# A two-layer graph attention kernel: one table of node products with three bf16 rows per node, one window load and one matmul per edge group, buffers 42 wide

## The chip, the cores and the metric

The kernel runs on one core of one Trainium2 chip. The metric is the device time of one execution in microseconds (us). TensorE is called PE, VectorE DVE, ScalarE ACT, GpSimd POOL and SyncE SP; PEld is PE's loading of weights. SP, ACT and POOL also issue DMAs.

## What is computed

A graph has 6250 nodes and 106250 edges (17 per node: 50000 random pairs in both directions, and one loop at each node). Edges are sorted by their target `dst`. Two attention layers follow one another, and the result is normalised. Cut to what matters:

```python
def egat(x, e, src, dst, W_ni, W_nj, W_fij, W_node, attn):
    f = (x @ W_ni.T)[src] + (x @ W_nj.T)[dst] + e @ W_fij.T      # per edge, 128 wide
    f = leaky_relu(f, 0.2)
    score = f @ attn
    a = softmax of score over the edges with the same dst
    return segment_sum((x @ W_node.T)[src] * a[:, None], dst), f

h0, h1 = egat(x, edge, src, dst, layer 1 weights)
h0 = relu(h0) + x;  h1 = relu(h1) + edge
h0b, _ = egat(h0, h1, src, dst, layer 2 weights)
out = layernorm(x + (h0b + x))
```

All inputs are f32.

## The kernel before, in words

Edges are cut into tiles of 128, groups of `TG` = 4 tiles (512 edges, `W`) and chunks of `GC` = 8 groups. There are 26 chunks (`CH`), 208 groups (`NG`) in each layer. Everything is kept transposed: features on the 128 partitions, edges along the row.

The stages are: (1) `project`, 13 slabs of 512 nodes: the product x @ W_nj, written to DRAM in bf16 parts; (2) layer 1; (3) `middle`, again 13 slabs: h0 from the sums, its rows to DRAM (`h0rows`) and its product for layer 2; (4) layer 2; (5) `end`, the layer norm.

*The product in bf16 parts.* One f32 number is written as up to three bf16 numbers (high, middle, low) that add up to it. ACT casts the high part (L314), DVE subtracts it (L332), ACT casts the rest to the middle part (L319), DVE subtracts again to get the low part (L337). High and low lie side by side in the table `projHL`, 256 numbers per node; the middle part lies in `projM`, 128 per node. ACT issues the two stores of a slab one after the other (L323, L325), with its row copy for the middle stage (L587) behind them. SP and POOL wait until all stores of a stage have landed before they read what depends on them.

*A group in a layer.* Because edges are sorted, a group touches a short run of target nodes, the window. SP loads for each group: its edge features (L383), the place of each edge's target in the window, spread over the partitions (`rel_bc`, L386), and the window's rows: 64 nodes of `projHL` (L388) and 64 nodes of `projM`, which go to partitions 64 to 127 of the same buffer (L390). It runs up to three groups ahead. In layer 1 it also stores h1 (L407). DVE compares `rel_bc` with `iota_win`, which holds the window place that each partition stands for (0 to 63 and 0 to 63 again), and makes a 0/1 matrix `onehot` (L974). PE then sums in PSUM bank bZ: W_fij times edges (L641), the window times onehot: high and middle parts at once over 128 partitions (L644), the low parts over 64 (L645), and W_ni times the source features (L652).

The source features come from POOL: 4 indirect gathers per group, each of 128 rows of x (or h0rows) named by `src`, into `xsrc` (L502). xsrc has three buffers of one chunk each. A gather into a buffer waits until PE has aggregated the same group of the chunk three back (`num_made`). PE transposes the gathered rows (L634), ACT copies them to SBUF (L565). ACT copies z from PSUM (L554), DVE makes fT (L1024) and in layer 1 h1 (L1028), PE multiplies by attn (L662). A chunk's scores go through the softmax on DVE, with short PE transposes in between (L685 to L699), while the next chunk's groups are in work.

*Aggregation*, two chunks behind: DVE builds for two groups at once a matrix `amat` of 8 tiles of 64 columns: 1 where an edge's target is the column's node (L939), times the edge's weight (L941). PE multiplies each tile of gathered rows with its 64 columns (L676), and DVE adds the 64 columns to the node sums `numT` (L957).

*What sets the order.* Each engine has its own instruction list, written out by hand; semaphores tie them. In a turn over a chunk PE does for each group g: z sum, scores of g-1, transposes of g+1, aggregation of group g two chunks back, softmax pieces. After the last gather of a layer two turns more, with aggregation alone for 16 groups, drain it.

All this is the narrow branch. It is taken when no group spans 64 nodes or more (`fits`, L816). Otherwise a wide branch runs, which treats each tile of 128 edges by itself with three parts and 128 columns. The profile shows the narrow one.

Of the kernel before, what the change touches and what calls it, by code (L numbers as in the profile page):

```python
# [9 lines left out]
WIN = 64  # L39
# [14 lines left out]
class Layer:  # L54


    def __init__(self, sem, gathered, n, edges_in, proj_hl, proj_m, table, h1_out):
        self.n = n
        self.edges_in, self.proj_hl, self.proj_m = edges_in, proj_hl, proj_m
# [54 lines left out]
def program(nc, eT, xT, xrows, idxT, dstT, dstR, dst8, ends, w_fij1, w_ni1, w_nj1, w_node1, attn1,  # L114
# [6 lines left out]
    projHL = [nc.dram_tensor(f"projHL{n}", [NP, 2 * D], bf16, kind="Internal").ap() for n in (1, 2)]  # L121
    projM = [nc.dram_tensor(f"projM{n}", [NP, D], bf16, kind="Internal").ap() for n in (1, 2)]
# [6 lines left out]
    with ctx:  # L129
# [6 lines left out]
        def sem(name):  # L136
# [7 lines left out]
        win_off = sb("win_off", [P, 1])  # L144
# [18 lines left out]
        group_row = sb("group_row", [1, NG], i32)  # L163
        cont = sb("cont", [1, NT + 1])
# [24 lines left out]
        apair = [a[:, :, :].rearrange("p i (h j) -> p (i h) j", j=WIN) for a in amat]  # L189
# [69 lines left out]
        L1 = Layer(sem, gathered, 1, eT, projHL[0], projM[0], xrows, h1T)  # L259
        L2 = Layer(sem, gathered, 2, h1T, projHL[1], projM[1], h0rows, None)  # L260
# [47 lines left out]
        def act_parts(act, made, parts, table_hl, table_m, m, q, t, lag):  # L308

            if reached(m, lag) and not (isinstance(m, int) and m >= NS + lag):  # L310
                k, s, u, w = back(m, q, t, lag)
                act.wait_ge(made, k + 1)
                above(act, parts.stored[u], w * 32)
                nc.scalar.copy(part_hl[u][:, :, 0, :], bAG[s][:, :].rearrange("p (b d) -> p b d", d=P)  # L314
                               ).then_inc(parts.high, 1)
            if reached(m, lag + 1) and not (isinstance(m, int) and m >= NS + lag + 1):
                k, s, u, w = back(m, q, t, lag + 1)
                act.wait_ge(parts.rest, k + 1)
                nc.scalar.copy(part_m[u], rest[s][:, :, :]).then_inc(parts.middle, 1)  # L319
            if reached(m, lag + 2):  # L320
                k, s, u, w = back(m, q, t, lag + 2)
                act.wait_ge(parts.low, k + 1)
                act.dma_start(rows4(table_hl, k), part_hl[u].rearrange("p b h d -> p b (h d)")  # L323
                              ).then_inc(parts.stored[u], 16)
                act.dma_start(rows4(table_m, k), part_m[u]).then_inc(parts.stored[u], 16)  # L325

        def dve_parts(dve, parts, m, q, t, lag):
            if reached(m, lag) and not (isinstance(m, int) and m >= NS + lag):
                k, s, u, w = back(m, q, t, lag)
                above(dve, parts.low, k - 1)  # L330
                dve.wait_ge(parts.high, k + 1)
                nc.vector.tensor_tensor(rest[s][:, :, :], bAG[s][:, :].rearrange("p (b d) -> p b d", d=P),  # L332
                                        part_hl[u][:, :, 0, :], ALU.subtract).then_inc(parts.rest, 1)
            if reached(m, lag + 1):
                k, s, u, w = back(m, q, t, lag + 1)
                dve.wait_ge(parts.middle, k + 1)
                nc.vector.tensor_tensor(part_hl[u][:, :, 1, :], rest[s][:, :, :], part_m[u], ALU.subtract  # L337
                                        ).then_inc(parts.low, 1)
# [3 lines left out]
        def _(sp):  # L342
# [24 lines left out]
            def load_layer(L, narrow):  # L367
                def first_nodes(row, at, count):
                    _, first = nc.values_load_multi_w_load_instructions(
                        row[0:1, bass.ds(at, count)], engines=(SP_,), min_val=0, max_val=N,  # L370
                        skip_runtime_bounds_check_because=SORTED)
                    return first

                def chunk(c):
                    if narrow:
                        first = first_nodes(group_row, c * GC, GC)
                    for g in range(GC):
# [7 lines left out]
                        if narrow:  # L385
                            sp.dma_start(rel_bc[q][:, :], relrow_g[bass.ds(n, 1), :].partition_broadcast(P)  # L386
                                         ).then_inc(L.loaded[q], 16)
                            sp.dma_start(window[q][0:WIN, 0:2, :].rearrange("p h d -> p (h d)"),  # L388
                                         L.proj_hl[bass.ds(first[g], WIN), :]).then_inc(L.loaded[q], 16)
                            sp.dma_start(window[q][WIN:2 * WIN, 0, :], L.proj_m[bass.ds(first[g], WIN), :]  # L390
                                         ).then_inc(L.loaded[q], 16)
                        else:
                            first = first_nodes(base_row, n * TG, TG)
                            sp.dma_start(rel_bc[q][:, :], relrow[bass.ds(n, 1), :].partition_broadcast(P)
                                         ).then_inc(L.loaded[q], 16)
                            for i in range(TG):
                                sp.dma_start(window[q][:, 3 * i:3 * i + 2, :].rearrange("p h d -> p (h d)"),
                                             L.proj_hl[bass.ds(first[i], P), :]).then_inc(L.loaded[q], 16)
                                sp.dma_start(window[q][:, 3 * i + 2, :], L.proj_m[bass.ds(first[i], P), :]
                                             ).then_inc(L.loaded[q], 16)  # L400
# [29 lines left out]
            for q in range(4):  # L430
                sp.wait_ge(p_parts.stored[q], 32 * slot_uses[q])
# [19 lines left out]
            for q in range(4):  # L451
                sp.wait_ge(m_rows_stored[q], 16 * slot_uses[q])
                sp.wait_ge(m_parts.stored[q], 32 * slot_uses[q])
# [22 lines left out]
        def _(pool):  # L476
# [11 lines left out]
            def layer(L):  # L488
# [18 lines left out]
                for c in range(XB):  # L507
                    if L.n == 1 and c == 2:
                        pool.wait_ge(p_made, NS)
                        for q in range(4):  # L510
                            pool.wait_ge(p_parts.stored[q], 32 * slot_uses[q])
# [9 lines left out]
            for q in range(4):  # L521
                pool.wait_ge(m_rows_stored[q], 16 * slot_uses[q])
                pool.wait_ge(m_parts.stored[q], 32 * slot_uses[q])
# [4 lines left out]
        def _(act):  # L528
# [6 lines left out]
            def project(m, s, q, t):  # L535
                act_parts(act, p_made, p_parts, projHL[0], projM[0], m, q, t, 0)
# [44 lines left out]
            def middle(m, s, q, t):  # L581
                act_parts(act, m_proj, m_parts, projHL[1], projM[1], m, q, t, 1)
# [26 lines left out]
        def _(pe):  # L609
# [14 lines left out]
            def layer(L, narrow):  # L624
                ready = 64 if narrow else 160
# [11 lines left out]
                def z_sum(c, g):  # L637
# [160 lines left out]
        def _(dve):  # L798
# [13 lines left out]
            v.tensor_copy(group_row[0:1, :], base_row[0:1, ::TG])  # L812
            v.memset(fits[:, :], 0)
# [15 lines left out]
            step(v.tensor_scalar(win_off[:, :], iota_col[:, :], WIN - 0.5, -float(WIN), ALU.is_gt, ALU.mult))  # L829
            step(v.tensor_tensor(iota_win[:, :], iota_col[:, :], win_off[:, :], ALU.add))  # L830
# [14 lines left out]
            def layer(L, narrow):  # L845
                one = L.h1_out is not None
                step = Steps(dve, L.dve_step)
                ready = 64 if narrow else 160
# [297 lines left out]
```

## Time and profile before

| | |
|---|---|
| median of 3 runs | 2458.83 us (2458.59 to 2458.99) |
| profiled execution, span | 2465.0 us |
| PE busy | 2248.0 us (91%) |
| PEld busy | 1337.3 us (54%) |
| DVE busy | 1421.2 us (58%) |
| ACT busy | 582.8 us (24%) |
| POOL busy | 1718.2 us (70%) |
| mean granted PE clock | 0.962 of 2.4 GHz |

The span is that of one profiled execution, from its first to its last instruction; no other time of that execution is recorded. It stands 6.2 us above the median of the runs without a profile. Busy shares are means over the span. An engine may be idle between two of its instructions for an issue gap, in which it waits for nothing, or for a wait on another engine or a DMA; the rows below name which.

### The profile page before, as it was taken

How to read it: one execution, taken by the hardware profiler on the slowest of the kernel's cores; microseconds unless marked ns; L12 is line 12 of the kernel's file. 1: busy time of each engine (PE TensorE's matmuls, PEld its weight loads, DVE VectorE, ACT ScalarE, POOL GpSimd, SP SyncE). 2: the span in 40 equal slices, each digit the busy share in tenths (PEclk: the TensorE clock that was granted, in tenths of full speed). 3: DMA queues.
4: the chain of work that ended last, by engine and by line, in shares of the span. 5: the costliest groups of instructions: out<-in, count | busy, mean ns of one | idle time of the engine just before them, and what ended most of it. 6: DMA issues, size and time to landing. Idle time of an engine off the chain costs nothing.

```text
span 2465.0 us, 46255 instructions
## 1 busy us (share of the span) xinstructions
PE 2248.0 (91%) x11602; PEld 1337.3 (54%) x11804; DVE 1421.2 (58%) x4210; ACT 582.8 (24%) x1120; POOL 1718.2 (70%) x1725
## 2 busy tenths in 40 slices
PE   3899999999999999999858999999999999999985
PEld 3455555555555555555634555555555555555562
DVE  5466666666666666666534555455555555554555
ACT  2222222222222222221222222222222222222213
POOL 6777777777777777775067777777777777777720
PEclk8999999999999999999789999999999999999976
DMA  7766666665556555564464444444444444444413
GB/s 224 215 194 186 186 186 185 186 184 180 173 177 181 175 178 172 175 180 133 136 170 131 129 136 133 122 136 134 129 134 130 134 128 134 128 135 128 135 38 96
DMA packets 318230, 378.84 MB, mean 154 GB/s; under 512 B 98892, under 2 KB 206006, under 8 KB 318128
## 3 DMA queue, kind: packets, MB, share of 16 engines
q1 hardware_dynamic: 235935, 257.64, 34.4%
q0 software_dynamic: 53328, 109.58, 16.6%
q10 hardware_dynamic: 28896, 10.75, 1.7%
q8 instruction: 35, 0.57, 0.1%
q14 instruction: 36, 0.29, 0.0%
HBM read 305.96 MB, written 71.78 MB: 153 GB/s over the span
## 4 chain that ended last, share of the span: by engine, by line
PE 40%; POOL 35%; issue 14%; DMA 6%; DVE 3%; ACT 1%; POOLq 0%; ACTq 0%; SPq 0%; DVEq 0%
POOL xsrc L502 35%; PE bZ L652 8%; PE bAG L676 8%; PE bZ L641 8%; PE bSC L662 7%; PE bXT L634 5%; PE bZ L645 3%; DMA xsrc<-h0rows,idx_slot 2%; DMA projM<-h 1%; DMA xsrc<-xT 1%; DMA xsrc<-xrows,idx_slot 1%; PE bZ L644 1%; DVE amat L939 0%; DVE amat L941 0%; ACT xsrc L601 0%
## 5 line engine op out<-in xcount | busy, mean ns | idle before, releaser
L502 POOL DMA_INDIRECT xsrc<-xrows,idx_slot x832 | 862.9, 1037 | 269.3 <-issue 241.4
L502 POOL DMA_INDIRECT xsrc<-h0rows,idx_slot x832 | 839.8, 1009 | 269.9 <-issue 239.7
L1024 DVE SCALAR_TENSOR_TENSOR fT<-zc 128x512 f32<-128x512 f32 x416 | 288.6, 694 | 590.5 <-ACT zc L554 553.4
L554 ACT COPY zc<-bZ 128x512 f32<-128x512 f32 x416 | 243.8, 586 | 1118.4 <-PE bZ L652 1104.1
L662 PEld LDWEIGHTS bSC<-fT,attn_at 128*32 128x32 f32 x3328 | 330.3, 110 | 317.0 <-issue 316.6
L652 PE MATMUL bZ<-xsT,wts 128*128 128x512 f32 x832 | 473.6, 651 | 0.0
L641 PE MATMUL bZ<-edge_in,wts 128*128 128x512 f32 x832 | 466.4, 643 | 7.5 <-DMA window<-projM 7.5
L676 PE MATMUL bAG<-amat,xsrc 128*128 128x64 f32 x3328 | 442.2, 279 | 8.6 <-DVE amat L941 8.3
L662 PE MATMUL bSC<-fT,attn_at 128*32 128x128 f32 x3328 | 442.3, 276 | 0.0
L676 PEld LDWEIGHTS bAG<-amat,xsrc 128*128 128x128 f32 x3328 | 425.9, 201 | 12.1 <-DVE amat L941 10.9
L634 PE MATMUL bXT<-ident,xsrc 128*128 128x128 f32 x1664 | 274.3, 288 | 101.9 <-DMA xsrc<-h0rows,idx_slot 61.6
L565 ACT COPY xsT<-bXT 128x512 f32<-128x512 f32 x416 | 243.9, 586 | 483.3 <-PE bXT L634 481.6
L634 PEld LDWEIGHTS bXT<-ident,xsrc 128*128 128x128 f32 x1664 | 176.2, 141 | 198.2 <-DMA xsrc<-h0rows,idx_slot 73.9
L645 PE MATMUL bZ<-onehot,window 64*128 64x512 bf16 x416 | 162.5, 391 | 31.5 <-issue 2.5
L645 PEld LDWEIGHTS bZ<-onehot,window 64*128 64x128 bf16 x416 | 38.5, 93 | 270.9 <-issue 270.9
L974 DVE TENSOR_SCALAR onehot<-rel_bc,iota_win 128x512 bf16<-128x512 bf16 x416 | 153.3, 369 | 41.9 <-issue 27.5
L652 PEld LDWEIGHTS bZ<-xsT,wts 128*128 128x128 f32 x832 | 125.1, 190 | 95.8 <-issue 95.8
L939 DVE TENSOR_TENSOR amat<-iota_row,relc 128x512 f32<-128x512 f32 x208 | 144.2, 693 | 11.4
L941 DVE TENSOR_TENSOR amat<-amat,wcol 128x512 f32<-128x512 f32 x208 | 145.0, 697 | 7.1
L1028 DVE SCALAR_TENSOR_TENSOR h<-zc,edge_in 128x512 f32<-128x512 f32 x208 | 142.7, 686 | 0.0
L641 PEld LDWEIGHTS bZ<-edge_in,wts 128*128 128x128 f32 x832 | 126.2, 191 | 17.1 <-DMA window<-projM 7.9
L957 DVE TENSOR_TENSOR numT<-numT,bAG 128x64 f32 x416 | 86.0, 207 | 75.6 <-PE bAG L676 61.2
(134 smaller groups left out, 1190.4 us busy)
## 6 DMA issues: line engine op xcount, KB each, us to landing
edge_in<-eT SPq DMA_DIRECT2D x208, 256.0 KB
rel_bc<-relrow_g SPq DMA_DIRECT2D x416, 128.0 KB
h1T<-h SPq DMA_DIRECT2D x208, 256.0 KB
edge_in<-h1T SPq DMA_DIRECT2D x208, 256.0 KB
xsrc<-xrows,idx_slot POOLq DMA_INDIRECT x832
window<-projHL SPq DMA_DIRECT2D x416, 32.0 KB
xsrc<-h0rows,idx_slot POOLq DMA_INDIRECT x832
xsrc<-xT SPq DMA_DIRECT2D x39, 256.0 KB, 3.4
```

The costliest lines, as they stand in the source:

```text
L502: pool.indirect_dma_start(xsrc[b][:, i, :], None, L.table, bass.IndirectOffsetOnAxis(ap=idx_slot[b][:, i:i + 1], axis=0)).then_inc(L.gathe ...
L554: nc.scalar.copy(zc[s][:, :], bZ[s][:, :]).then_inc(L.z_copied, 1)
L565: nc.scalar.copy(xsT[s][:, :], bXT[:, :]).then_inc(L.xt_copied, 1)
L634: last = tp(bXT[:, i * P:i * P + P], xsrc[b][:, g * TG + i, :], ident[:, :])
L641: mm(bZ[s][:, :], fij, edge_in[q][:, :], start=True, stop=False)
L645: mm(bZ[s][:, :], window[q][0:WIN, 1, :], onehot[s][0:WIN, :], start=False, stop=False)
L652: last = mm(bZ[s][:, :], ni, xsT[s][:, :], start=False, stop=True)
L662: last = mm(bSC[0:TC, 0:P], attn_at[:, L.n - 1, TC - 1 - t:2 * TC - 1 - t], fT[s][:, i * P:i * P + P], start=t == 0, stop=t == TC - 1)
L676: last = mm(bAG[s][:, 0:WIN], rows, apair[g // 2 % 2][:, g % 2 * TG + i, :], start=i == 0, stop=i == TG - 1)
L941: v.tensor_tensor(a, a, of(wcol), ALU.mult).then_inc(L.a_made, 1)
L974: v.tensor_scalar(onehot[s][:, :], rel_bc[q][:, :], (iota_win if narrow else iota_col)[:, 0:1], None, ALU.is_equal).then_inc(L.onehot_made, 1)
L1024: v.scalar_tensor_tensor(fT[s][:, :], zc[s][:, :], SLOPE, zc[s][:, :], ALU.mult, ALU.max).then_inc(L.f_made, 1)
```

## The change

The two tables become one, `proj`, of 3 x 128 bf16 numbers per node: high, middle, low. Read as a table of 128-number rows it has three rows per node, and a window of 42 nodes is 126 rows; the load takes 128 rows from row 3 x (first node) on, one to each partition. `part_row` holds the first nodes times three. `iota_win` becomes the partition number divided by three, rounded down, so that one matmul with onehot sums all three parts. The window width `WIN` goes from 64 to 42, and with it the columns of amat, of the aggregation matmuls and of the sums into numT; `fits` now asks for less than 42 nodes.

The three parts of a slab lie in one buffer and are stored by one DMA. Two of the four slab buffers move from xsrc[2] to h1[2] and h1[3]. The waits count 48 in place of 64 for a group's loads and 16 in place of 32 for a slab's stores. The wide branch loads a tile's window in one DMA in place of two; its matmuls are as before.

```diff
-WIN = 64
+WIN = 42
...
-    projHL = [nc.dram_tensor(f"projHL{n}", [NP, 2 * D], bf16, kind="Internal").ap() for n in (1, 2)]
-    projM = [nc.dram_tensor(f"projM{n}", [NP, D], bf16, kind="Internal").ap() for n in (1, 2)]
+    proj = [nc.dram_tensor(f"proj{n}", [NP, 3 * D], bf16, kind="Internal").ap() for n in (1, 2)]
...
-        apair = [a[:, :, :].rearrange("p i (h j) -> p (i h) j", j=WIN) for a in amat]
+        apair = [a[:, :, :].rearrange("p i j -> p (i j)")[:, 0:2 * TG * WIN].rearrange("p (h j) -> p h j", j=WIN)
+                 for a in amat]
...
-        slab = [xsrc[2][:, q * TG:(q + 1) * TG, :].rearrange("p b d -> p (b d)") for q in range(4)]
-        part_hl = [xsrc[2][:, (4 + q) * TG:(5 + q) * TG, :].rearrange("p b d -> p (b d)").bitcast(bf16)
-                   .rearrange("p (b h d) -> p b h d", h=2, d=P) for q in range(4)]
-        part_m = [h1[2 + q // 2][:, q % 2 * (W // 2):(q % 2 + 1) * (W // 2)].bitcast(bf16)
-                  .rearrange("p (b d) -> p b d", d=P) for q in range(4)]
+        flat2 = xsrc[2][:, :, :].rearrange("p b d -> p (b d)")
+        parts_w = 3 * W // 2
+        part = [flat2[:, q * parts_w:(q + 1) * parts_w].bitcast(bf16)
+                .rearrange("p (b h d) -> p b h d", h=3, d=P) for q in range(4)]
+        slab = [flat2[:, 4 * parts_w + q * W:4 * parts_w + (q + 1) * W] for q in range(2)] + [h1[2][:, :], h1[3][:, :]]
...
-                act.dma_start(rows4(table_hl, k), part_hl[u].rearrange("p b h d -> p b (h d)")
+                act.dma_start(rows4(table, k), part[u].rearrange("p b h d -> p b (h d)")
                               ).then_inc(parts.stored[u], 16)
-                act.dma_start(rows4(table_m, k), part_m[u]).then_inc(parts.stored[u], 16)
...
-                            sp.dma_start(window[q][0:WIN, 0:2, :].rearrange("p h d -> p (h d)"),
-                                         L.proj_hl[bass.ds(first[g], WIN), :]).then_inc(L.loaded[q], 16)
-                            sp.dma_start(window[q][WIN:2 * WIN, 0, :], L.proj_m[bass.ds(first[g], WIN), :]
-                                         ).then_inc(L.loaded[q], 16)
+                            sp.dma_start(window[q][:, 0, :], L.proj.rearrange("n (h d) -> (n h) d", h=3)[
+                                bass.ds(first[g], P), :]).then_inc(L.loaded[q], 16)
...
                         mm(bZ[s][:, :], window[q][:, 0, :], onehot[s][:, :], start=False, stop=False)
-                        mm(bZ[s][:, :], window[q][0:WIN, 1, :], onehot[s][0:WIN, :], start=False, stop=False)
...
+            v.tensor_scalar(part_row[0:1, :], base_row[0:1, ::TG], 3, None, ALU.mult)
...
-            step(v.tensor_scalar(win_off[:, :], iota_col[:, :], WIN - 0.5, -float(WIN), ALU.is_gt, ALU.mult))
-            step(v.tensor_tensor(iota_win[:, :], iota_col[:, :], win_off[:, :], ALU.add))
+            thirds = amat[0][:, 0, 0:WIN]
+            step(v.tensor_scalar(thirds, iota_row[:, 1:WIN + 1], 3.0, iota_col[:, 0:1], ALU.mult, ALU.is_le))
+            step(v.tensor_reduce(iota_win[:, :], thirds, mybir.AxisListType.X, ALU.add))
```

PE's list in the loop over a layer's groups, one group, before (the names are those of the section on the kernel; L662 is the group before, L676 the chunk two back):

```order
L641 MATMUL bZ<-edge_in,wts 128x512
L644 MATMUL bZ<-onehot,window 128x512
L645 MATMUL bZ<-onehot,window 128x512
L652 MATMUL bZ<-xsT,wts 128x512
L662 MATMUL bSC<-fT,attn_at 32x128 x4
L634 MATMUL bXT<-ident,xsrc 128x128 x4
L676 MATMUL bAG<-amat,xsrc 128x64 x4
```

And after:

```order
L607 MATMUL bZ<-edge_in,wts 128x512
L610 MATMUL bZ<-onehot,window 128x512
L617 MATMUL bZ<-xsT,wts 128x512
L627 MATMUL bSC<-fT,attn_at 32x128 x4
L600 MATMUL bXT<-ident,xsrc 128x128 x4
L641 MATMUL bAG<-amat,xsrc 128x42 x4
```

The second onehot matmul is gone, and the aggregation has 42 columns; nothing else moves.

ACT's list in the middle stage, one slab, before (CAST makes the parts, COPY is the row copy):

```order
L314 CAST xsrc<-bAG 128x4x128
L319 CAST h_2<-amat 128x512
L323 ISA
L323 DMA projHL<-xsrc 128x4x256
L325 ISA
L325 DMA projM<-h_2 128x4x128
L587 COPY xsrc<-bXT 128x512
```

And after:

```order
L285 CAST xsrc<-bAG 128x4x128
L290 CAST xsrc<-amat 128x4x128
L294 ISA
L294 DMA proj<-xsrc 128x4x384
L553 COPY xsrc<-bXT 128x512
```

The row copy now has one DMA issue ahead of it in place of two.

## Rows read from the trace of the kernel before

**Rows 1.** The page's chain that ended last, shares of the span by engine.

```profile
PE 40%; POOL 35%; issue 14%; DMA 6%; DVE 3%; ACT 1%; POOLq 0%; ACTq 0%; SPq 0%; DVEq 0%
```

**Rows 2.** Groups: line, engine, out<-in, form, xcount | busy us, mean ns | idle before.

```profile
L502 POOL DMA_INDIRECT xsrc<-xrows,idx_slot x832 | 862.9, 1037 | 269.3 <-issue 241.4
L502 POOL DMA_INDIRECT xsrc<-h0rows,idx_slot x832 | 839.8, 1009 | 269.9 <-issue 239.7
...
L676 PEld LDWEIGHTS bAG<-amat,xsrc 128*128 128x128 f32 x3328 | 425.9, 201 | 12.1 <-DVE amat L941 10.9
...
L939 DVE TENSOR_TENSOR amat<-iota_row,relc 128x512 f32<-128x512 f32 x208 | 144.2, 693 | 11.4
...
L925 DVE TENSOR_TENSOR wcol<-bSM,rcol 128x32 f32<-128x32 f32 x52 | 9.9, 191 | 1.8
```

**Rows 3.** Gathers by tile: ns min/median/max, first and last start us.

```profile
L502 POOL DMA_INDIRECT xsrc<-xrows,idx_slot x832: 948/955/1721, 10.0 to 1149.7; - x167
L502 POOL DMA_INDIRECT xsrc<-h0rows,idx_slot x832: 948/955/1492, 1245.1 to 2358.6; - x167
```

**Rows 4.** POOL's waits: us in total, times, longest us.

```profile
POOL xsrc L502 <- issue: 481.1, 1572, 1.2
POOL idx_slot L493 <- DMA projM<-h: 93.5, 1, 93.5
...
POOL xsrc L502 <- PE bAG L676: 13.7, 43, 0.9
```

**Rows 5.** Timeline, POOL and DVE: start us, us, instruction, idle before it.

```profile
604.54 0.68 DVE L1028 SCALAR_TENSOR_TENSOR h<-zc,edge_in 128x512 f32<-128x512 f32 x1
604.83 1.22 POOL L502 DMA_INDIRECT xsrc<-xrows,idx_slot  x1 [0.30 <-issue]
...
607.51 0.69 DVE L939 TENSOR_TENSOR amat<-iota_row,relc 128x512 f32<-128x512 f32 x1
...
607.61 1.42 POOL L502 DMA_INDIRECT xsrc<-xrows,idx_slot  x1 [0.30 <-issue]
```

**Rows 6.** Gathers alone by stretch: us, POOL busy (count), PE clock, DMA share, GB/s.

```profile
140.00:540.00 400.00, 299.31 (x292) 1.00 0.61 186
540.00:1140.00 600.00, 455.77 (x438) 1.00 0.59 177
```

**Rows 7.** Timeline of PE over one group of layer 1.

```profile
603.21 1.06 PE L662 MATMUL bSC<-fT,attn_at 128*32 128x128 f32 x8
...
607.03 0.39 PE L645 MATMUL bZ<-onehot,window 64*128 64x512 bf16 x1
607.35 1.13 PE L652 MATMUL bZ<-xsT,wts 128*128 128x512 f32 x2
608.40 1.06 PE L662 MATMUL bSC<-fT,attn_at 128*32 128x128 f32 x8
```

**Rows 8.** Timeline of POOL at the start of chunk 3.

```profile
141.79 0.43 POOL L493 COPY idx_slot<-idx_all 128x32 int32 x1 [1.36 <-PE bAG L676]
```

**Rows 9.** Behind layer 1's last gather: one piece of the chain, then PE's timeline.

```profile
1158.33 0.54 PE bZ L645
...
1176.66 1.97 PE L676 MATMUL bAG<-amat,xsrc 128*128 128x64 f32 x8 [0.57 <-DVE amat L941]
...
1193.34 3.67 PE L676 MATMUL bAG<-amat,xsrc 128*128 128x64 f32 x16 [0.23 <-DVE amat L941]
```

**Rows 10.** Middle stage: timeline of ACT, then the chain at its end.

```profile
1220.29 0.59 ACT L587 COPY xsrc<-bXT 128x512 f32<-128x512 f32 x1 [0.24 <-issue]
...
1238.78 1.37 ACTq L323
...
1240.18 3.84 DMA projM<-h
```

**Rows 11.** PE's timeline in layer 2, and its slice (clock behind POOL's count).

```profile
1337.00 1.12 PE L634 MATMUL bXT<-ident,xsrc 128*128 128x128 f32 x4 [2.42 <-DMA xsrc<-h0rows,idx_slot]
...
1330.00:1340.00 10.00, 7.41 (x28) 3.67 (x28) 4.59 (x16) 1.76 (x3) 7.56 (x9) 0.84 0.45 132
```

More of the change, by code:

```diff
@@ L54, with __init__ @@
 class Layer:
-    def __init__(self, sem, gathered, n, edges_in, proj_hl, proj_m, table, h1_out):
+    def __init__(self, sem, gathered, n, edges_in, proj, table, h1_out):
         self.n = n
-        self.edges_in, self.proj_hl, self.proj_m = edges_in, proj_hl, proj_m
+        self.edges_in, self.proj = edges_in, proj
         self.table, self.h1_out = table, h1_out
@@ L163, in program @@
         group_row = sb("group_row", [1, NG], i32)
+        part_row = sb("part_row", [1, NG], i32)
         cont = sb("cont", [1, NT + 1])
@@ L258, in program @@
         gathered = [[sem(f"gathered{b}_{g}") for g in range(GC)] for b in range(XB)]
-        L1 = Layer(sem, gathered, 1, eT, projHL[0], projM[0], xrows, h1T)
-        L2 = Layer(sem, gathered, 2, h1T, projHL[1], projM[1], h0rows, None)
+        L1 = Layer(sem, gathered, 1, eT, proj[0], xrows, h1T)
+        L2 = Layer(sem, gathered, 2, h1T, proj[1], h0rows, None)
         four = lambda name: [sem(f"{name}{q}") for q in range(4)]
@@ L306, in back, with act_parts @@
             return m - by, (q - by) % 2, (q - by) % 4, t if q >= by else t - 1
-        def act_parts(act, made, parts, table_hl, table_m, m, q, t, lag):
+        def act_parts(act, made, parts, table, m, q, t, lag):
             if reached(m, lag) and not (isinstance(m, int) and m >= NS + lag):
@@ L312, in act_parts @@
                 act.wait_ge(made, k + 1)
-                above(act, parts.stored[u], w * 32)
-                nc.scalar.copy(part_hl[u][:, :, 0, :], bAG[s][:, :].rearrange("p (b d) -> p b d", d=P)
+                above(act, parts.stored[u], w * 16)
+                nc.scalar.copy(part[u][:, :, 0, :], bAG[s][:, :].rearrange("p (b d) -> p b d", d=P)
                                ).then_inc(parts.high, 1)
@@ L318, in act_parts @@
                 act.wait_ge(parts.rest, k + 1)
-                nc.scalar.copy(part_m[u], rest[s][:, :, :]).then_inc(parts.middle, 1)
+                nc.scalar.copy(part[u][:, :, 1, :], rest[s][:, :, :]).then_inc(parts.middle, 1)
             if reached(m, lag + 2):
@@ L332, in dve_parts @@
                 nc.vector.tensor_tensor(rest[s][:, :, :], bAG[s][:, :].rearrange("p (b d) -> p b d", d=P),
-                                        part_hl[u][:, :, 0, :], ALU.subtract).then_inc(parts.rest, 1)
+                                        part[u][:, :, 0, :], ALU.subtract).then_inc(parts.rest, 1)
             if reached(m, lag + 1):
@@ L336, in dve_parts @@
                 dve.wait_ge(parts.middle, k + 1)
-                nc.vector.tensor_tensor(part_hl[u][:, :, 1, :], rest[s][:, :, :], part_m[u], ALU.subtract
+                nc.vector.tensor_tensor(part[u][:, :, 2, :], rest[s][:, :, :], part[u][:, :, 1, :], ALU.subtract
                                         ).then_inc(parts.low, 1)
@@ L367, in load_layer, with first_nodes @@
             def load_layer(L, narrow):
-                def first_nodes(row, at, count):
+                def first_nodes(row, at, count, most):
                     _, first = nc.values_load_multi_w_load_instructions(
-                        row[0:1, bass.ds(at, count)], engines=(SP_,), min_val=0, max_val=N,
+                        row[0:1, bass.ds(at, count)], engines=(SP_,), min_val=0, max_val=most,
                         skip_runtime_bounds_check_because=SORTED)
@@ L375, in chunk @@
                     if narrow:
-                        first = first_nodes(group_row, c * GC, GC)
+                        first = first_nodes(part_row, c * GC, GC, 3 * N)
                     for g in range(GC):
@@ L387, in chunk @@
                                          ).then_inc(L.loaded[q], 16)
-                            sp.dma_start(window[q][0:WIN, 0:2, :].rearrange("p h d -> p (h d)"),
-                                         L.proj_hl[bass.ds(first[g], WIN), :]).then_inc(L.loaded[q], 16)
-                            sp.dma_start(window[q][WIN:2 * WIN, 0, :], L.proj_m[bass.ds(first[g], WIN), :]
-                                         ).then_inc(L.loaded[q], 16)
+                            sp.dma_start(window[q][:, 0, :], L.proj.rearrange("n (h d) -> (n h) d", h=3)[
+                                bass.ds(first[g], P), :]).then_inc(L.loaded[q], 16)
                         else:
-                            first = first_nodes(base_row, n * TG, TG)
+                            first = first_nodes(base_row, n * TG, TG, N)
                             sp.dma_start(rel_bc[q][:, :], relrow[bass.ds(n, 1), :].partition_broadcast(P)
@@ L396, in chunk @@
                             for i in range(TG):
[L397 to L400, printed above, removed]
+                                sp.dma_start(window[q][:, 3 * i:3 * i + 3, :].rearrange("p h d -> p (h d)"),
+                                             L.proj[bass.ds(first[i], P), :]).then_inc(L.loaded[q], 16)
                         if L.h1_out is not None and not (isinstance(c, int) and n < GS):
@@ L430, in _ @@
             for q in range(4):
-                sp.wait_ge(p_parts.stored[q], 32 * slot_uses[q])
+                sp.wait_ge(p_parts.stored[q], 16 * slot_uses[q])
             sp.wait_ge(graph_in, 16 * 5)
@@ L452, in _ @@
                 sp.wait_ge(m_rows_stored[q], 16 * slot_uses[q])
-                sp.wait_ge(m_parts.stored[q], 32 * slot_uses[q])
+                sp.wait_ge(m_parts.stored[q], 16 * slot_uses[q])
             either(L2)
@@ L510, in layer @@
                         for q in range(4):
-                            pool.wait_ge(p_parts.stored[q], 32 * slot_uses[q])
+                            pool.wait_ge(p_parts.stored[q], 16 * slot_uses[q])
                     chunk(c, c, False)
@@ L522, in _ @@
                 pool.wait_ge(m_rows_stored[q], 16 * slot_uses[q])
-                pool.wait_ge(m_parts.stored[q], 32 * slot_uses[q])
+                pool.wait_ge(m_parts.stored[q], 16 * slot_uses[q])
             layer(L2)
@@ L535, in project @@
             def project(m, s, q, t):
-                act_parts(act, p_made, p_parts, projHL[0], projM[0], m, q, t, 0)
+                act_parts(act, p_made, p_parts, proj[0], m, q, t, 0)
             slabs(act, project)
@@ L624, in layer @@
             def layer(L, narrow):
-                ready = 64 if narrow else 160
+                ready = 48 if narrow else 96
                 fij, ni = wts[:, (L.n - 1) * 4 + FIJ, :], wts[:, (L.n - 1) * 4 + NI, :]
```

5 lines of the change are left out of this document (2 added, 3 removed).

## The prediction

> **What bounds the kernel now.** I read the chain of waits first. It puts 40% on TensorE (PE), 35% on GpSimd's (POOL's) gathers and 14% on issue [rows 1], so it does not choose: in a layer it goes back and forth between two engines that run at nearly one pace. The second look is POOL's own instructions. Each layer has 832 gathers, and they lie in one unbroken row, from 10.0 to 1149.7 us and from 1245.1 to 2358.6 us [rows 3]. Between two of them stands a constant 0.30 us that waits for nothing. Of POOL's idle time ahead of a gather 481.1 us is that, and only 13.7 us, spread over 43 places, is put down to PE [rows 4]; with 0.30 us of issue in each place nothing real is left of it. There is one true wait for PE, of 1.36 us at 141.79 us [rows 8]. So a layer lasts as long as 832 times a gather and its gap: 1149.7 + 0.95 - 10.0 = 1140.6 us or 5.48 us per group of 4 in layer 1, and likewise 1114.5 us or 5.36 in layer 2.
>
> The third look is PE's own pace. From the score matmuls of one group to those of the next it needs 608.40 - 603.21 = 5.19 us when it waits for no data [rows 7]. PE is the faster engine by 0.2 to 0.3 us per group. The bound is POOL, and PE's busy share of 91% in the table only says that the other engine is close.
>
> The fourth look is why gathers differ in length. The shortest and the median one take 948 and 955 ns [rows 3], the mean is 1037 and 1009 ns [rows 2]: over the floor stand 862.9 - 832 x 0.948 = 74.2 us in layer 1 and 839.8 - 788.7 = 51.1 us in layer 2. The longer gathers have a VectorE (DVE) instruction under their start: the one at 607.61 took 1.42 us under an amat instruction of 607.51 to 608.20, the one at 604.83 took 1.22 us under an h instruction of 604.54 to 605.22 [rows 5]. In both the excess over 0.948 is the time left of the DVE instruction less 0.12 us (0.59 - 0.12 = 0.47; 0.39 - 0.12 = 0.27). Laid over all 1664 gathers in the timeline the rule holds to 0.01 us: a gather touches something 0.12 us after its start, and if a DVE instruction whose inputs both come from SBUF (fT, h, or either of the two that make amat) is running then, it waits for that one's end. Counted so, the amat pair holds up 152 gathers for 43.2 us in all, fT and h the others for 65 us.
>
> **The change, part by part.**
>
> *The second one-hot matmul goes* (416 of them). It moves the next matmul by 607.35 - 607.03 = 0.32 us [rows 7], so PE's group falls from 5.19 to 4.87 us: 133 us of PE work. In the steady loop all of it lies beside POOL, whose 5.36 to 5.48 us per group go on. Next late is the same gather as before; PE waits longer for it. On the path it counts in three places. POOL's one wait of 1.36 us [rows 8] goes, since PE has 16 groups x 0.32 us = 5 us in hand by then: -1.4. In the drain behind each layer's last gather it stands once, for 0.54 us at the slow clock [rows 9]. And PE catches up with POOL earlier in layer 1. There a gather costs 299.31/292 = 1.025 us while PE lags and 455.77/438 = 1.041 us once the two are locked [rows 6]; PE was level by about 540 us and will be by about 250, so some 215 gathers get 0.016 us longer: +3.
>
> *amat shrinks from 512 to 336 columns.* An f32 DVE instruction takes 191 ns at 32 columns and 693 at 512 [rows 2], 1.05 ns a column (both instructions of the pair take the same within 4 ns), so each of 416 falls to an estimated 0.51 us. The delay that it causes grows with its length twice, by the chance to be hit and by what is left when hit: 43.2 x (1 - (0.51/0.693)^2) = 43.2 x 0.46 = 20 us less. This is the largest term, and it is on the path, since POOL is. Its bounds are 0 (DVE is tied to POOL by the landing of each group, so hits need not be random) and 43 (none is left). I take 20, because the 152 hits lie all over the range of offsets.
>
> Here a rule of the Trainium skill speaks against the term. "SBUF — State Buffer", section "Who interferes with whom", says that a tensor_tensor with two SBUF inputs takes only the read side of the pair that DVE shares with GpSimd, and infers that it does not stall descriptor generation. By it the 20 would be 0. The rows show the reverse.
>
> *The 42-column aggregation matmuls* replace 64-column ones. Their cost is the weight load, 201 ns of PEld each, all of it kept [rows 2]: 0. The sum into numT is 22 columns narrower: 0.02 us off DVE, beside PE.
>
> *The drain of each layer* (16 groups of aggregation alone) goes by pairs: numT, the amat pair, two groups of matmuls. At the end a pair takes 3.90 us, 3.67 of them PE and 0.23 a wait for amat [rows 9]. With amat 0.37 us shorter that wait goes, and PE bounds there: 4 pairs x 0.23. Three earlier pairs wait longer than 0.37, the shortest 0.57 [rows 9], and give it whole: 1.1. With the 0.54 above 2.5 per layer: -5, between 0 and -8.
>
> *The projections are stored by one DMA in place of two* (13 slabs in each of two stages). The first stage runs beside gathers from the input, and POOL's only wait for such a store is the 93.5 us between the layers [rows 4]: hidden, and so are the two or three small DVE instructions more, which stand beside it. The middle stage is on the path: POOL's first gather of layer 2 waits for its last store. ACT's row copy waits behind the second issue for 0.24 us, in a row of the four slabs that the chain goes through [rows 10]: about 1. At the end the second DMA starts 1.40 us behind the first, and its landing of 3.84 us is what POOL waits for [rows 10]; one DMA starts where the first did: 1.4. Together -2.5, bounds 0 and -6.
>
> *The window loads* are one DMA of 128 rows of 256 B for two, 64 rows each; SP issues one fewer per group. The loads run three groups ahead. Nothing on the path, +0 to +2 if landings of gathers are crowded.
>
> *Sum against the profiled execution:* -20 - 1.4 - 5 - 2.5 + 3 = -26, so a span of 2439. The span of 2465.0 stands 6.2 us above the median of 2458.83, hence **2433 us**.
>
> **Rivals.**
>
> *Delays only change place.* The hits on gathers do not follow amat's length, because fT and h start 0.32 us earlier against POOL and take more of them. Then -1.4 - 5 - 2.5 and a contention term of -5 to +5 are left: about 2450. For it: fT and h carry 65 us, against 43 of amat. Against it: nothing makes their hits more likely than now.
>
> *PE is the bound after all*, as 40% of the chain could be read. Then 416 x 0.32 = 133 us go: 2326. POOL's unbroken rows speak against it.
>
> *Slower: PE falls to its slow clock between gathers.* PE will wait in every group, 0.5 us and more. One wait of 2.42 us at 1337.00 is followed by transposes of 1.12 us where 0.66 is usual; the granted clock of that slice is 0.84, full speed of 2.4 GHz mixed with 1.2 [rows 11]. It came back at once, and POOL never noticed, because PE may lag by some seven groups. A group at 1.2 GHz costs PE about twice 4.87, 9.7 us, as an estimate from the clock's two levels. POOL's 5.4 us are passed when more than (5.4 - 4.87)/(9.7 - 4.87) = one group in nine is slow, and then POOL stalls for PE. One in seven would make 4.87 + 4.83/7 = 5.56 us per group, 0.14 more than the 5.42 of now, or 58 us over 416 groups, less the 9 us of the ends: about 2508. Against it: PE that lags has no waits, and so gets its clock back.
>
> The Trainium skill describes this in "TensorE: Matmul & The Clock Gate", section "HAM oscillation": matmuls that wait for a DMA in every tile can start every tile slow. By that rule the time is the 2508 of this rival.
>
> *The change does not do what it says:* if one group spanned 42 nodes or more, the wide branch would run, with 12 small matmuls per group. There are 17 edges per node, so 512 edges span 30 nodes on average, and the drawn input's widest group spans 34. Chance 1%.
>
> **Chances.** Forecast 62% (own range 2415 to 2446), delays only change place 24% (2444 to 2458), PE the bound 3%, slow clock 8%, another loss 3%. The 80% range leaves out PE as bound, the slow clock and the ends: 2411 to 2454. It takes in the amat term from 0 to 43. A measurement of this kernel tells 0.2%, 4.9 us, from no change. Faster by more than that: 62 + 3 + most of the 24, 0.85. Within it: 0.06. Slower: 0.09.
>
> **What would show it.** In the changed profile: gathers still in one row, with the span of a layer over 208 near 5.42 and 5.31 us; their mean at about 1.02 and 1.00 us; amat at 0.51 us; PE busy less, near 86%, with 0.3 us more of waiting for gathers per group, and its clock still near 1.0 in the layers; 45 us in place of 47 between the last gather and the first middle matmul; the wait of POOL in the middle shorter than 93.5 by 5. Wrong would be amat at 0.51 us with the mean of a gather unchanged (first rival), or POOL with long waits for PE (third).

## The result, and the profile after

The changed kernel takes **2419.6 us** (median of 4 runs, 2414.8 to 2426.7) where the kernel before takes 2458.9 (2458.6 to 2463.6): a ratio of 0.983, 95% interval 0.981 to 0.986. The forecast was 2433 with a range of 2411 to 2454. The direction and the bound were right; the gain is 39 us where 26 were summed. The spread of the runs (12 us) is wider than that of the kernel before (5 us).

The two profiled executions differ by more than the medians, 2465.0 against 2415.3 us or 49.7, because that of before lies above its median and that of after below its own. Terms are compared on these spans below, verdicts on medians.

The page of the changed kernel, its shares and its chain by engine:

```profile
PE 2083.7 (86%) x11186; PEld 1346.9 (56%) x11388; DVE 1336.3 (55%) x4211; ACT 580.6 (24%) x1120; POOL 1679.3 (70%) x1725
...
POOL 52%; issue 22%; PE 16%; DMA 6%; DVE 2%; POOLq 1%; ACT 1%; SPq 0%; DVEq 0%; ACTq 0%
```

With 164 us less of busy time on PE the chain no longer wavers between two engines [rows 1]: POOL and the issue gaps, nearly all of them ahead of a gather, are 74% of it. The groups of gathers and of amat, then the gathers by tile, then POOL's waits:

```profile
L468 POOL DMA_INDIRECT xsrc<-xrows,idx_slot x832 | 842.6, 1013 | 269.3 <-issue 243.2
L468 POOL DMA_INDIRECT xsrc<-h0rows,idx_slot x832 | 823.4, 990 | 269.7 <-issue 244.1
...
L906 DVE TENSOR_TENSOR amat<-iota_row,relc 128x336 f32<-128x336 f32 x208 | 106.0, 510 | 11.4
```

```profile
L468 POOL DMA_INDIRECT xsrc<-xrows,idx_slot x832: 947/952/1670, 9.8 to 1125.6; - x167
L468 POOL DMA_INDIRECT xsrc<-h0rows,idx_slot x832: 947/952/1683, 1215.4 to 2312.4; - x167
```

```profile
POOL xsrc L468 <- issue: 487.3, 1593, 1.2
POOL idx_slot L459 <- DMA proj<-xsrc: 87.9, 1, 87.9
...
POOL xsrc L468 <- PE bAG L641: 8.2, 23, 0.9
```

Still one unbroken row of gathers in each layer, still the same floor of 0.947 to 0.948 us. What changed is the excess over the floor [rows 2, 3]. amat takes 0.51 us, as estimated. PE's wait for gathers is what grew: 229.9 us in 244 places in place of 93.9 in 123.

Where the 49.7 us of span went: layer 1's row of gathers 23.9 (1140.6 to 1116.7), layer 2's 16.5 (1114.4 to 1097.9), from layer 1's last gather to layer 2's first 5.6 (94.5 to 88.9), from layer 2's last gather to the end 3.4 (105.4 to 102.0), the start 0.2.

### The profile page after: what moved, and what is told of

Its sections match the earlier page's. It is cut to its first block, busy times and chain, and to the rows that moved or that the text cites. A ratio compares the mean times of both kernels' runs of the same rounds, so it can differ in the third digit from the quotient of the medians.

```text
span 2415.3 us, 44118 instructions
## 1 busy us (share of the span) xinstructions
PE 2083.7 (86%) x11186; PEld 1346.9 (56%) x11388; DVE 1336.3 (55%) x4211; ACT 580.6 (24%) x1120; POOL 1679.3 (70%) x1725
## 4 chain that ended last, share of the span: by engine, by line
POOL 52%; issue 22%; PE 16%; DMA 6%; DVE 2%; POOLq 1%; ACT 1%; SPq 0%; DVEq 0%; ACTq 0%
POOL xsrc L468 52%; PE bAG L641 4%; PE bZ L607 3%; PE bZ L617 3%; PE bSC L627 2%; PE bXT L600 2%; DMA xsrc<-h0rows,idx_slot 2%; DMA xsrc<-xrows,idx_slot 2%; DMA proj<-xsrc 1%; DMA h<-xT 1%; PE bZ L719 0%; DMA xsrc<-xT 0%; PE bAG L725 0%; PE bZ L610 0%; ACT xsrc L567 0%
## 5 line engine op out<-in xcount | busy, mean ns | idle before, releaser
L468 POOL DMA_INDIRECT xsrc<-xrows,idx_slot x832 | 842.6, 1013 | 269.3 <-issue 243.2
L607 PE MATMUL bZ<-edge_in,wts 128*128 128x512 f32 x832 | 483.1, 664 | 6.0 <-DMA window<-proj 6.0
L617 PE MATMUL bZ<-xsT,wts 128*128 128x512 f32 x832 | 445.2, 618 | 13.9 <-issue 4.2
L641 PE MATMUL bAG<-amat,xsrc 128*128 128x42 f32 x3328 | 437.2, 285 | 4.8 <-DVE amat L908 4.5
L617 PEld LDWEIGHTS bZ<-xsT,wts 128*128 128x128 f32 x832 | 166.3, 200 | 160.2 <-issue 140.0
L924 DVE TENSOR_TENSOR numT<-numT,bAG 128x42 f32 x416 | 76.9, 185 | 119.9 <-PE bAG L641 111.4
L906 DVE TENSOR_TENSOR amat<-iota_row,relc 128x336 f32<-128x336 f32 x208 | 106.0, 510 | 11.4
L908 DVE TENSOR_TENSOR amat<-amat,wcol 128x336 f32<-128x336 f32 x208 | 105.9, 509 | 7.2
L610 PEld LDWEIGHTS bZ<-onehot,window 128*128 128x128 bf16 x416 | 41.8, 100 | 104.5 <-issue 102.1
L610 PE MATMUL bZ<-onehot,window 128*128 128x512 bf16 x214 | 83.4, 390 | 0.0
```

Of the source, the lines that this page charges most:

```text
L468: pool.indirect_dma_start(xsrc[b][:, i, :], None, L.table, bass.IndirectOffsetOnAxis(ap=idx_slot[b][:, i:i + 1], axis=0)).then_inc(L.gathe ...
L607: mm(bZ[s][:, :], fij, edge_in[q][:, :], start=True, stop=False)
L617: last = mm(bZ[s][:, :], ni, xsT[s][:, :], start=False, stop=True)
L641: last = mm(bAG[s][:, 0:WIN], rows, apair[g // 2 % 2][:, g % 2 * TG + i, :], start=i == 0, stop=i == TG - 1)
```

## The experiments

Theory A: the time is POOL's row of gathers, and the gain is mostly that amat holds gathers up for less. Theory B: the gain is the removed matmul. Theory C: it is the DMAs, fewer and smaller. Theory D, for the last experiment: any long DVE instruction holds a gather up, whatever it reads.

**Two kinds of sets.** Each set of runs has its own kernel before. In three sets (e1 to e4; e5; f2, f3 and f5), here called the waiting ones, the kernel before itself takes 3016 to 3051 us, at a mean granted clock of 0.87 to 0.89. In the profiles of these sets ScalarE (ACT), DVE and POOL wait for things that the profile does not name: in e1 175, 191 and 155 times, for 4.8, 3.0 and 2.0 us on average and 33 at the longest. In the other sets (f1, g2, g3, g5), here the quiet ones, the kernel before takes 2457 to 2462 us at a clock of 0.96 to 0.97. Why there are two kinds stays open. That it is the chip isn't shown: the recorded chip number is 0 for f5 and also, 22 minutes later, for g5. Nor is it shown whether the lower clock is a cause of the waits or follows from them. The quiet sets are compared with the result above. The waiting ones are told because they teach something else.

### amat 64 wide again (e1, f1)

```diff
 the changed kernel
 WIN = 42
+AW = 64
...
-                            last = mm(bAG[s][:, 0:WIN], rows, apair[g // 2 % 2][:, g % 2 * TG + i, :],
+                            last = mm(bAG[s][:, 0:AW], rows, apair[g // 2 % 2][:, g % 2 * TG + i, :],
...
-                        step(v.tensor_tensor(a, iota_row[:, 0:WIN].unsqueeze(1).broadcast_to(both), of(relc),
+                        step(v.tensor_tensor(a, iota_row[:, 0:AW].unsqueeze(1).broadcast_to(both), of(relc),
```

The shapes of `a`, of apair and of the sums into numT follow; the window load stays at 42 nodes.

> The changed kernel with one part undone: amat, the aggregation matmuls and the sums into numT are 64 columns wide again; the table, the single window load and the single one-hot matmul stay. Theory A (the gain is mostly shorter hold-ups of gathers by the amat pair, 43.2 us before and 16.1 after): amat back at 0.69 us, the mean gather back near 1.02 to 1.03 us over both layers, about 27 us of hold-ups and 2 to 4 us in the drains come back: 2450 us (2442 to 2456). Theory B (the gain is the removed matmul): no change from the changed kernel, 2420. Theory C (fewer and smaller DMAs): no change either, 2420.

> The same kernel as e1_amat64, wanted beside a kernel before of 2459 us. Theory A: 2450 us (2442 to 2456), mean gather near 1.02 to 1.03 us. Theories B and C: 2420 us. Beside a kernel before of about 3030 us: near 0.971 of it, as measured there.

Measured, f1: 2461.8 us beside 2462.5, ratio 1.000 (0.999 to 1.002). The one table and the removed matmul by themselves bring nothing. Theories B and C, each as the whole cause, fall in the quiet sets. The time is 6 us above theory A's range. The profile of f1 shows what came back: amat's hold-ups (44.0 us), and fT and h hold up for 73.7 us, where the profile of the changed kernel has 59.5. The profiled execution took 2469.5 us, 8 above the median of f1, so a part of the 73.7 may belong to this one execution. Its gathers:

```profile
L469 POOL DMA_INDIRECT xsrc<-xrows,idx_slot x832 | 866.9, 1042 | 269.4 <-issue 245.1 <-POOL idx_slot L460 21.5 <-PE bAG L642 2.7
L469 POOL DMA_INDIRECT xsrc<-h0rows,idx_slot x832 | 842.5, 1013 | 269.9 <-issue 244.9 <-POOL idx_slot L460 22.9 <-PE bAG L642 2.1
```

The means of 1042 and 1013 ns are those of before, 1037 and 1009 [rows 2].

### amat 42 wide alone (e2, f2, g2)

The mirror image: the kernel before, with `WIN` at 64 for the tables, windows and matmuls, and 42 in the same four places (amat, its shape, aggregation, sums into numT).

> The kernel before with one part of the change alone: amat, aggregation and sums 42 columns wide; two tables, two window loads and two one-hot matmuls as before. Theory A: hold-ups by amat fall from about 43 to 16 us and the drains by 2 to 4 us in all: 2429 us (2422 to 2438). Theory B and theory C: 2459 us, no change from before.

> The kernel before with amat, aggregation and sums 42 wide, nothing else; wanted beside a kernel before of 2460 us. After f1, where the rest of the change gave nothing, theory A in its sharper form says that amat's width alone carries the whole of the change: 2420 to 2426 us, mean gather near 1.00 us. Theories B and C: 2460.

> The same kernel as e2_amat42_alone: the kernel before with amat, aggregation and sums 42 wide, wanted beside a kernel before of 2460 us. With g3 (amat 42, the one table, the matmul's work back) at 2431.6, what differs here is the table alone, worth 2 to 5 us in the middle stage: theory A 2434 us (2428 to 2440). Theories B and C: 2460. If amat's width carried the whole change, as f1 by itself would say: 2420.

Measured, g2: 2435.3 us (2431.9 to 2437.9) beside 2459.1, ratio 0.990 (0.989 to 0.992). amat's width alone is worth 24 us, inside what theory A said (2434). It is not the whole of the change, which the sharper form in f2 and g2 would have had at 2420. The runs of f2 and e2 are in waiting sets and could not test this.

### The matmul's work put back (e3, f3, g3)

```diff
 the changed kernel
                         mm(bZ[s][:, :], window[q][:, 0, :], onehot[s][:, :], start=False, stop=False)
+                        mm(bZ[s][:, :], zero_w[:, :], onehot[s][0:64, :], start=False, stop=False)
```

`zero_w` is a tile of 64 x 128 bf16 zeros, so PE does the work and adds nothing.

> The changed kernel with the work of the second one-hot matmul put back: per group one more bf16 matmul of 64 partitions by 512 columns, with a weight tile of zeros, so it adds nothing. Theory A: PE's 0.32 us per group lie beside POOL in the layers, only the two drains and the start of chunk 3 feel it: 2422 us (2418 to 2428), PE busy near 91% again. Theory B: 2459 us or more. Theory C: 2420.

> The changed kernel with the matmul of zeros put back (see e3_matmul_back), beside a kernel before of 2460 us. Theory A: 2420 to 2428 us with PE busy near 91%. Theory B: 2455 or more.

> The same kernel as e3_matmul_back and f3_matmul_back (the changed kernel with the work of the second one-hot matmul put back), wanted beside a kernel before of 2460 us. Theory A: 2420 to 2428 us, PE busy near 91%. Theory B: 2455 or more. After f1 there is a third: f1 came out 12 us above its expectation, so the locking of PE to POOL may cost something in itself; if so, a busier PE would bring 2410 to 2418.

Measured, g3: 2431.6 us (2429.6 to 2435.4) beside 2460.5, ratio 0.989 (0.986 to 0.992). That is 12 us above the changed kernel, where theory A had 2: its range ended at 2428. Theory B's 2455 is far off too, and so is the third one, 2410 to 2418. What the table adds to g2 is 4 us, and the two intervals overlap, so it is not clear of noise. By the profile the 12 us are again gathers: amat holds them up for 16.1 us, as in the changed kernel, but fT and h for 73.5 in place of 59.5.

```profile
L469 POOL DMA_INDIRECT xsrc<-xrows,idx_slot x832 | 848.9, 1020 | 269.4 <-issue 237.0 <-POOL idx_slot L460 18.8 <-PE bAG L643 13.7
L469 POOL DMA_INDIRECT xsrc<-h0rows,idx_slot x832 | 832.0, 1000 | 269.9 <-issue 244.9 <-POOL idx_slot L460 22.9 <-PE bAG L643 2.1
```

### The table alone (e4)

e1 and e3 together: amat 64 wide and the matmul of zeros.

> Both of the former together: the changed kernel with amat 64 columns wide and the matmul of zeros back. What is left of the change is the one table with its single window load per group and single store per slab. Theory A: only the middle stage gains, about 2.5 us, and the layers are as before: 2454 us (2448 to 2460). Theory B: 2459. Theory C (the DMAs are the gain): 2420 to 2425.

It ran only in a waiting set: 3006.8 us beside 3050.6, ratio 0.985 (0.982 to 0.988). The ratio is from five runs of 2992 to 3013 us; a sixth took 5377 us, and why is open. This answers another question than the one asked. The chain of its profile:

```profile
PE 53%; another core or an unknown queue 28%; issue 10%; ACT 3%; DVE 2%; DMA 2%; ACTq 0%; SPq 0%; DVEq 0%; POOL 0%; POOLq 0%
```

POOL is at 0% in it; it waits for aggregation and for unnamed things in some 240 places. There PE and the unnamed waits are the bound, and the parts of the change trade places: the table alone brings 1.5%; table and matmul together (e1) 2.9% (0.968 to 0.974); amat's width alone costs 0.3% (e2, 1.001 to 1.006) or does nothing (f2, 1.000 to 1.005); table and amat (e3, f3) 1.0 and 1.4%. Here, other than in the quiet sets, the removed matmul and the table pay and amat's width does not, as theories B and C had it. The changed kernel itself did not run in such a set, and what the engines wait for there stays open; the profile names no source.

### fT and h read z from PSUM (e5, f5, g5)

```diff
 the changed kernel
                     above(pe, L.z_copied, n - 1)
+                    above(pe, L.f_made, n - 1)
+                    if L.h1_out is not None:
+                        above(pe, L.h1_made, n - 1)
...
-                            v.scalar_tensor_tensor(fT[s][:, :], zc[s][:, :], SLOPE, zc[s][:, :], ALU.mult, ALU.max
+                            v.scalar_tensor_tensor(fT[s][:, :], bZ[s][:, :], SLOPE, zc[s][:, :], ALU.mult, ALU.max
...
-                                v.scalar_tensor_tensor(h1[q][:, :], zc[s][:, :], 0.0, edge_in[q][:, :],
+                                v.scalar_tensor_tensor(h1[q][:, :], bZ[s][:, :], 0.0, edge_in[q][:, :],
```

> The changed kernel, where the two other instructions that hold up gathers, fT and h, take z from PSUM for one of their inputs: fT reads bZ and zc in place of zc twice, h reads bZ and the edge features. Each then has one input from SBUF and the same length. PE waits for both before it writes the bank again. Theory A (a gather that touches SBUF waits for a DVE instruction with two SBUF inputs): where the changed kernel takes 2420 us, the 59.5 us of hold-ups by fT and h go, the 16 of amat stay: mean gather near 0.96 to 0.98 us in both layers, 2420 - 55 = 2365 us (2355 to 2380), PE coming close to being the bound. Theory D (any DVE instruction of that length holds a gather up, whatever its inputs): 2420, no change. The same in the other kind of run, in which the kernel before takes 3050 us and engines wait for things the profile does not name: theory A says a few us there, since POOL does not run in one row; theory D none.

> The changed kernel with z read from PSUM by fT and h (see e5_z_from_psum), beside a kernel before of 2460 us. Theory A: the 59.5 us of hold-ups by fT and h go: 2365 us (2355 to 2380), mean gather 0.96 to 0.98 us. Theory D (inputs do not matter, only length): 2420, hold-ups by fT and h as before.

> The same kernel as e5_z_from_psum and f5_z_from_psum, in both of which the hold-ups of gathers by fT and h were gone (mean gather 0.96 to 0.97 us) but engines waited beside for things that the profile does not name. Wanted beside a kernel before of 2460 us. Theory A: about 2365 us (2355 to 2380). Theory D: 2420. If PE, and not POOL, takes over as the bound, the time stays above 2380 with POOL waiting for aggregation.

Measured, g5: **2361.5 us** (2357.6 to 2362.5) beside 2456.8, ratio 0.961 (0.959 to 0.962), 58 us below the changed kernel. Theory A's 2365 is met, theory D falls. Both instructions are as long as before, and the hold-ups of gathers by them fall from 59.5 to 0.6 us. The timelines can be counted gather by gather: of those that begin between 0.06 us after the start of fT or h and 0.18 us before its end, the changed kernel holds up all 207, and in g5 the longest excess among 178 is 0.03 us. The added waits of PE for fT and h do not explain that, since in the same execution of g5 all 69 that begin so under an amat instruction are held up. The groups, and one place in the timeline:

```profile
L468 POOL DMA_INDIRECT xsrc<-xrows,idx_slot x832 | 807.9, 971 | 269.5 <-issue 244.3
L468 POOL DMA_INDIRECT xsrc<-h0rows,idx_slot x832 | 803.6, 966 | 269.9 <-issue 246.2
L994 DVE SCALAR_TENSOR_TENSOR fT<-bZ,zc 128x512 f32<-128x512 f32 x416 | 287.8, 692 | 513.1 <-ACT zc L520 490.0
```

```profile
834.11 0.69 DVE L994 SCALAR_TENSOR_TENSOR fT<-bZ,zc 128x512 f32<-128x512 f32 x1 [1.79 <-ACT zc L520]
834.29 0.95 POOL L468 DMA_INDIRECT xsrc<-xrows,idx_slot  x1 [0.30 <-issue]
```

This gather starts 0.18 us into an fT of 0.69 and takes the floor. Before, a gather that began 0.29 us into h took 1.22 [rows 5]. In the waiting sets the same kernel brings 2.2 and 2.4% (e5, f5), less than e1's 2.9%, with the same short gathers (f5):

```profile
L468 POOL DMA_INDIRECT xsrc<-xrows,idx_slot x832 | 805.2, 968 | 459.6 <-issue 220.3 <-remote 144.9 <-PE bAG L644 78.2
```

The mechanism works there too, but a gather is not the bound; POOL waits longer instead.

The rule has an edge that is not settled. onehot reads one wide input from SBUF and the column `iota_win`, and it holds gathers up as well: 31 of 37 that begin so under it in g5, by 0.13 us at most, 3 us in all.

### All of them side by side

| kernel | median us | its before | span of the profile | held up by amat | by fT and h |
|---|---|---|---|---|---|
| before | 2458.9 | | 2465.0 | 43.2 | 65.3 |
| table, no second matmul (f1) | 2461.8 | 2462.5 | 2467.5 | 44.0 | 73.7 |
| amat 42 alone (g2) | 2435.3 | 2459.1 | 2434.6 | 15.5 | 73.9 |
| amat 42 and table (g3) | 2431.6 | 2460.5 | 2428.2 | 16.1 | 73.5 |
| the change, whole | 2419.6 | 2458.9 | 2415.3 | 16.2 | 59.5 |
| and z from PSUM (g5) | 2361.5 | 2456.8 | 2355.6 | 14.8 | 0.6 |

The two columns on the right are worked out from the timeline of each one's profiled execution: all gathers over the floor of 0.948 us whose start, 0.11 us in, falls into such an instruction, and their excess summed. They belong to the span beside them, not to the median.

## Why the prediction was right, step by step

**What bounds the kernel: right.** In six kernels the time follows the mean gather. g3 puts PE back to 92% busy, f1 leaves it at 85%, and f1 is the slower by 30 us.

**The rule of the hold-up: right.** The excess of a held gather is the rest of the DVE instruction less 0.12 us in every one of these profiles (0.11 to 0.14 for nine in ten, g5 aside, where hardly any by fT and h are left to test it), and g5 shows that for fT and h the second SBUF input is the condition. The Trainium skill, "SBUF — State Buffer", section "Who interferes with whom", infers that a tensor_tensor with two SBUF inputs does not stall descriptor generation. Read so, the amat term would be 0; its hold-ups fell by 27 us and g2's time by 24, and here the measurement decides.

**Its size: the right term, sized too small.** I took 20 us, 27 to 28 were measured, in each pairing (43.2 to 16.2, 43.2 to 15.5, 44.0 to 16.2). The failing step is "the delay grows with its length twice", with the whole length of 0.693 and 0.51 us. The longest hold-up by amat is 0.524 us at 64 columns and 0.329 at 42. A longest one of the changed kernel:

```profile
1430.42 0.51 DVE L908 TENSOR_TENSOR amat<-amat,wcol 128x336 f32<-128x336 f32 x1
1430.48 1.28 POOL L468 DMA_INDIRECT xsrc<-h0rows,idx_slot  x1 [0.30 <-issue]
```

An instruction holds up only what is left behind its first 0.05 us and ahead of its last 0.12: its length less 0.17 or 0.18. With that, 43.2 x (0.34/0.524)^2 = 18.2 would have been left, a gain of 25. The numbers for it stood in the rows: the excess of 0.47 at an overlap of 0.59 [rows 5].

**The locked stretch: wrong.** I added 3 us, for gathers that lengthen once PE is level with POOL [rows 6]. When that would be was right: once layer 1 has started, PE first waits for a gather at 561 us before, and at 220 after. The same view after:

```profile
140.00:540.00 400.00, 300.74 (x299) 0.99 0.62 183
540.00:1110.00 570.00, 429.18 (x427) 0.99 0.60 177
```

1.006 and 1.005 us: no difference, but PE is level in most of both stretches. The test is g3, where PE is level from 609 us on:

```profile
140.00:540.00 400.00, 301.24 (x295) 1.00 0.62 183
610.00:1110.00 500.00, 376.89 (x371) 1.00 0.60 176
```

1.021 us while PE lags and 1.016 once the two are level: nothing is added. The step took a difference of 0.016 us between two stretches of one execution for a law.

**Delays that change place: half right, of both signs.** As a rival it had 24% and a gather delayed elsewhere for each one spared. In fact what fT and h hold up differs by up to 14 us between these profiles, whichever way amat goes. With amat at 42, taking the matmul out shifts them from 73.5 to 59.5 us, and the time by 12; with amat at 64 the table and the matmul together leave them at 73.7 against 65.3, and bring nothing. Why a lighter PE helps in one and not in the other is not settled. The sums are of one execution each, and runs of the changed kernel alone spread over 12 us, those of g5, where fT and h hold nothing, over 5. Against the spans, on which the terms were summed, the forecast of 26 us is 24 short of 49.7. Of these, 7 are amat, 6 fT and h, 3 the locked stretch, and 1 the middle stage. The other 7 are small pieces: 4 in gathers that neither amat nor fT or h holds up, 2 in gaps ahead of layer 1's gathers, 1 in the rest. Against the medians only 13 are missing, since the span before stands 6 us above its median and the span after 4 below. That 2419.6 lies within the range of 2411 to 2454 owes something to the width of that range, which took in the amat term from 0 to 43.

**The ends: right.** Behind the last gathers, to the first matmul of the next stage, 44.9 and 43.9 us in place of 46.9 and 47.0: 5.1 together, forecast 5. At the end of the drain the wait for amat is gone; PE runs the last 9 groups through:

```profile
1154.55 16.09 PE L641 MATMUL bAG<-amat,xsrc 128*128 128x42 f32 x72
```

The middle stage, from there to layer 2's first gather, takes 44.1 in place of 47.6 us: 3.5, forecast 2.5. POOL's wait there fell from 93.5 [rows 4] to 87.9, forecast 5 less.

**PE's one wait at chunk 3: right,** 1.36 us [rows 8] are gone. The window loads of 256-byte rows show in nothing.

**The slow clock: did not bite.** PE's waits for gathers more than doubled (93.9 to 229.9 us), and the mean granted clock between 1400 and 2300 us fell from 0.99 to 0.96, so there are more spells at 1.2 GHz, some 8% of that time in place of 2 (an estimate from the clock's two levels). POOL waits for PE 8.2 us in all of the kernel. The buffer of three chunks swallows the spells, as the rival's counter-argument had it; one group in nine was not reached. The rival's 2508 us took one group in seven as slow, a share that no row gave. If every group were slow, as the rule named beside it would allow, PE's 9.7 us a group would make far more than 2508, so that time did not come out of the rule; neither was seen.

## What to carry to other kernels

Where two engines are nearly level, ask which one has no true waits in a whole stage; its row of instructions is the time, and the other's busy share is no guide. When GpSimd issues gathers, look for VectorE instructions with two SBUF inputs that run under them: each is a possible hold-up. Shorten it, or give it one input from PSUM, which left the time of fT and h at 0.69 us. And parts of a change do not add up: amat's width is worth 24 us by itself (g2) and 42 on top of the rest (f1 to the whole change); the table and the removed matmul are worth 0 by themselves and 16 on top of amat's width. They can even trade places: in the waiting sets table and removed matmul brought 2.9%, amat's width nothing.

## What the runs showed of the hardware

- A gather issued by GpSimd (128 rows) takes 0.947 us, with 0.30 us to the next. If it begins more than 0.05 us into a VectorE instruction with two f32 inputs from SBUF, it ends 0.83 us after that instruction's end instead. In the kernel before, all 387 gathers that began between 0.06 us into fT, h or amat and 0.18 us before its end were held up, with an excess within 0.03 us of this rule. With one input from PSUM and one from SBUF, at the same 0.69 us, the longest excess among 178 was 0.03 us (g5).
- The same program took 23 to 24% more in three sets of runs than in the others (3016 to 3051 against 2457 to 2462 us). In those sets ScalarE, VectorE and GpSimd waited 2 to 5 us at a time on average for things that the profile does not name (e1), at a lower granted clock (0.87 to 0.89 against 0.96 to 0.97). The shortest gather (0.946 to 0.949 us), fT (0.69) and the copy of z (0.59) kept their length.
